# First five ticks of a two-stage mixture-of-experts kernel written out one by one, its opening loads issued two at a time

## The reference

```python
x = x + _L0_xattn_ref(_layernorm(x), itok, ctx, ctx, ctx)   # stage 1
x = x + _L0_ffn_ref(_layernorm(x), router_w, wg, wu, wd)    # stage 2
```

## Time and profile before

| what | value |
|---|---|
| median of three runs | 255.06 us |
| the profiled execution's own time | 255.76 us |
| its span, first to last instruction | 253.8 us |
| TensorE, busy share of the span | 92% |
| VectorE, ScalarE, GpSimd, busy share | 86%, 83%, 65% |

### The profile page before, as it was taken

How to read it: one execution, slowest core, us unless ns; L and a number is a source line. 1 busy time by engine, 2 the same in 40 slices (tenths; PEclk the granted TensorE clock), 3 DMA queues, 4 the chain that set the end, 5 groups by cost and what they waited for, 6 DMA issues and landing times.

```text
span 253.8 us, 5722 instructions
## 1 busy us (share of the span) xinstructions
PE 234.7 (92%) x1409; PEld 172.4 (68%) x1419; DVE 218.2 (86%) x675; ACT 210.5 (83%) x324; POOL 164.2 (65%) x325
## 2 busy tenths in 40 slices
PE   2398999999999999999999999999999999999990
PEld 2255778888888888888888888886455555555530
DVE  5879989899889988799888988879999999999871
ACT  2767899799888988898888888787899999999960
POOL 4362665868778777588777664347538786757653
PEclk9999999999999999999999999999999999999996
DMA  5999944935754499784566534541388962211110
GB/s 203 425 359 362 424 180 151 362 131 226 243 210 146 134 354 406 283 324 157 201 249 227 147 127 169 207 146 69 98 237 250 310 251 85 83 41 68 70 37 0
DMA packets 13726, 51.71 MB, mean 204 GB/s; under 512 B 2750, under 2 KB 2750, under 8 KB 10112
## 3 DMA queue, kind: packets, MB, share of 16 engines
q1 hardware_dynamic: 8816, 37.91, 42.4%
q0 software_dynamic: 4880, 13.44, 14.4%
HBM read 40.49 MB, written 13.48 MB: 213 GB/s over the span
## 4 chain that ended last, share of the span: by engine, by line
PE 73%; DVE 10%; DMA 9%; issue 4%; ACT 1%; POOL 1%; SPq 0%; DVEq 0%; ACTq 0%
PE bank L1555 33%; PE bank L1677 19%; PE bank L1539 9%; PE bank L1647 5%; DMA staged<-weight_chunks 4%; PE bank L1669 4%; DMA ternary<-weight_chunks 3%; PE bank L1784 2%; DMA staged<-x_rows 1%; DVE ternary L957 1%; DVE ctx_lo L1000 1%; PE bank L1574 1%; POOL out_rows L643 1%; DVE ternary L1019 1%; DMA token_ids<-token_ids_in 1%
## 5 line engine op out<-in xcount | busy, mean ns | idle before, releaser
L1677 PE MATMUL bank<-ternary,qT 128*128 x179 | 43.6, 380 | 0.5
L694 ACT ACTIVATE ternary<-staged 128x2048 bf16<-128x2048 f32 x20 | 38.0, 1899 | 2.5 <-DMA staged<-weight_chunks 2.5
L700 ACT ACTIVATE ternary<-staged,w_scale 128x1536 int16<-128x1536 f32 x20 | 31.4, 1576 | 2.3 <-DVE w_scale L1014 0.6
L1677 PEld LDWEIGHTS bank<-ternary,qT 128*128 128x128 bf16 x184 | 17.7, 97 | 20.2 <-issue 5.4
L562 POOL DMA_INDIRECT x_rows<-row,store_at x19 | 25.5, 1340 | 6.8 <-POOL store_at L554 5.0
L643 POOL DMA_INDIRECT out_rows<-late_rows,late_token x18 | 19.0, 1057 | 9.4 <-DVE late_rows L1350 8.0
L473 POOL DMA_INDIRECT x<-x_rows,gather x16 | 18.5, 1155 | 10.2 <-DVE gather L969 6.3
L1677 PE MATMUL bank<-ternary,rT 128*128 x87 | 22.6, 380 | 0.4 <-ACT rT L812 0.2
L747 ACT ACTIVATE p<-bank,rstd 128x512 f32<-128x512 f32 x19 | 13.0, 684 | 11.6 <-PE bank L1555 11.5
L1555 PE MATMUL bank<-ctx_hi,pT_hi 128*128 x76 | 22.3, 415 | 0.1
L1555 PE MATMUL bank<-ctx_hi,hT_hi 128*128 x76 | 22.3, 414 | 0.0
(11 more groups left out here) (237 smaller groups left out, 658.6 us busy)
## 6 DMA issues: line engine op xcount, KB each, us to landing
staged<-weight_chunks SPq DMA_DIRECT2D x20, 1024.0 KB, 5.5
late_rows<-x_rows SPq DMA_DIRECT2D x18, 260.0 KB, 3.7
ternary<-ctx_chunks SPq DMA_DIRECT2D x4, 1024.0 KB, 8.3
ternary<-weight_chunks SPq DMA_DIRECT2D x4, 1024.0 KB, 9.8
x_rows<-filler SPq DMA_DIRECT2D x1, 2080.0 KB, 12.9
staged<-x_rows SPq DMA_DIRECT2D x5, 260.0 KB, 2.7
x_rows<-row,store_at POOLq DMA_INDIRECT x19, 6.0
out_rows<-late_rows,late_token POOLq DMA_INDIRECT x18
```

Of the source, the lines that this page charges most:

```text
L694: nc.scalar.activation(ternary[:, m * K * D:(m + 1) * K * D], staged_of(i), ACT.Abs, accum_out=abs_sum[:, 2 * i:2 * i + 1]).then_inc(abs_r ...
L700: nc.scalar.activation(ternary[:, m * K * D + DVE_COLS:(m + 1) * K * D].bitcast(I16), staged_of(i)[:, DVE_COLS:], ACT.Copy, scale=w_scale[ ...
L1677: last = pe.matmul(ps[:, :], left[:, k * P:(k + 1) * P], ternary[:, bass.ds(e * (3 * K * D) + (kind * K + k) * D, D)], start=(k == 0), sto ...
```

## The change

The loops of TensorE, VectorE and ScalarE now start at t = 5 (`OPENING`). What they did for t = 2 to 4, and blocks 0 and 1, stands written out in a new order. On TensorE other work is put between the parts of a product, by a table `ahead` from part number to a function. Blocks 0 to 3 (`b < E1`, E1 = 4) now wait for `hT_lo` only at the third part; block 4 and later still wait at the start. `second_product(0)` waits for the low half of pT only at its third part. SP waits until context 2 has landed before it issues matrix 3, and until matrix 2 has landed before context 3. One warm-up matmul of 12 is dropped. GpSimd's list is unchanged. No arithmetic is added or removed.

```diff
-WARM_UP = (9, 3)
+WARM_UP = (8, 3)
+OPENING = 5
...
             load_context(2)
             load_weights(2)
+            sp.wait_ge(ctx_in_sem[2], 16)
             load_weights(3)
+            sp.wait_ge(staged_early_in[0], 16)
             load_context(3)
...
# ScalarE
-            sum_abs(1)
             evict_hT(0)
             scale_part(0)
+            sum_abs(1)
+            evict_hT(1)
+            silu(0)
+            sum_abs(2)
+            evict_pT(0)
             scale_part(1)
...
-            for t in range(2, TICKS):
+            for t in range(OPENING, TICKS):
...
# VectorE, from block 2's statistics on
+            moments_of(2)
+            aggregate(2)
+            normalise(2)
+            gate(0)
+            hT_rest(1)
+            mean_of(1)
+            scale_of(1)
+            low_half(2, 0)
...
+            cut(4)
+            residual(2)
+            negative_mean(2)
+            scale_part(5)
+            hT_rest(4)
+            largest(1)
+            top_logits(1)
...
# TensorE
-                    if n == 1 and b == 1:
+                    if n == 1 and b is not None and 1 <= b < E1:
                         pe.wait_ge(ctx_lo_ready, e + 1)
-                    if n == 2 and b in (0, 1):
+                    if n in ahead:
+                        ahead[n]()
+                    if n == 2 and b is not None and b < E1:
                         pe.wait_ge(hT_lo_ready, b + 1)
...
-                if b < 2:
+                if b < E1:
                     pe.wait_ge(hT_hi_ready, b + 1)
...
                 else:
                     pe.wait_ge(hT_lo_ready, b + 1)
...
+            def in_second2():
+                rank(0)
+                sum_mean(5)
+                transpose_h(4)
+            second_product(2, {2: in_second2})
+            transpose_p(3)
+
+            def in_first4():
+                logits(1)
+            first_product(4, {2: in_first4})
+            load_expert(5)
+            count_in(0)
+            transpose_x1(2)
+            transpose_h(5)
+            rank(1)
+            sum_mean(6)
+            second_product(3)
+            logits(2)
+            count_in(1)
+            for t in range(OPENING, B1):
```

More of the change, by code:

```diff
@@ L1360, in _ @@
             normalise(0)
-            variance(0)
             low_half(0, 1)
[L1363 to L1366, removed]
+            scale_of(0)
             moments_of(1)
@@ L1369, in _ @@
             normalise(1)
+            hT_rest(0)
+            variance(0)
             variance(1)
-            scale_part(0)
-            gate(0)
-            hT_rest(1)
+            low_half(1, 0)
             low_half(1, 1)
-            scale_part(1)
-            pT_rest(0)
             moments_of(2)
@@ L1379, in _ @@
             normalise(2)
+            gate(0)
[3 more added lines that the diff above has]
+            low_half(2, 0)
             variance(2)
-            low_half(2, 0)
-            gate(1)
+            scale_part(0)
+            pT_rest(0)
+            low_half(2, 1)
             mean_of(2)
             scale_of(2)
-            hT_rest(2)
-            low_half(2, 1)
-            scale_part(2)
+            gate(1)
             moments_of(3)
             aggregate(3)
+            residual(0)
+            negative_mean(0)
+            hT_rest(2)
+            normalise(3)
             variance(3)
+            scale_part(1)
+            moments_of(4)
+            mean_of(3)
+            scale_of(3)
+            aggregate(4)
+            pT_rest(1)
+            gate(2)
+            low_half(3, 0)
+            low_half(3, 1)
+            mean_of(4)
+            scale_part(2)
+            scale_of(4)
+            residual(1)
+            negative_mean(1)
+            hT_rest(3)
+            scale_part(3)
+            scale_part(4)
+            top_logits(0)
+            choice(0)
+            one_hot(0)
+            pT_rest(2)
+            normalise(4)
+            largest(0)
+            moments_of(5)
+            variance(4)
+            mean_of(5)
+            gate(3)
+            scale_of(5)
+            row_index(0)
+            aggregate(5)
+            variance(5)
+            cut(4)
+            residual(2)
+            negative_mean(2)
+            scale_part(5)
+            hT_rest(4)
+            largest(1)
+            top_logits(1)
+            choice(1)
+            one_hot(1)
+            normalise(5)
+            pT_rest(3)
+            largest(2)
+            gate(4)
+            mean_of(6)
+            scale_of(6)
+            scale_part(6)
+            row_index(1)
+            hT_rest(5)
+            moments_of(6)
+            aggregate(6)
+            variance(6)
+            cut(5)
             early, factors = early_slots(), mean_products()
-            for t in range(2, TICKS):
+            for t in range(OPENING, TICKS):
                 interlude = early if t == EARLY_AFTER + 4 else iter(())
@@ L1583, in transpose_h, with first_product @@
                 transpose1(hT_ps, h).then_inc(hT_ready, 1)
[L1585 removed]
+            def first_product(b, ahead={}):
                 if not 0 <= b < B1:
                     return
[L1588 removed]
+                if b < E1:
                     pe.wait_ge(hT_hi_ready, b + 1)
[L1591 removed]
+                    pe.wait_ge(*((ctx_hi_ready, b + 1) if b < 2 else (pool_hi_ready, b - 1)))
                     pe.wait_ge(centred, 1)
```

104 lines of the change are left out of this document (63 added, 41 removed).

## The result

The changed kernel takes 260.87 us (median of four runs, 259.94 to 261.83) against 255.34 us before (four runs, 254.93 to 255.88): a ratio of 1.0215, 95% interval 1.0165 to 1.0265. It is slower, by some 2%. 255.5 us was forecast, with 256.7 as the upper end.

What follows compares the result with a forecast made beforehand. TensorE was taken as the bound, VectorE as a nearly full second; the start of tick 5 fixes the time. +0.3 and +0.15 give +0.45 us: 255.76 to 256.2 profiled, 255.5 us as median, range 254.3 to 256.7.

Steps and rivals of the forecast that it cites:

- VectorE from 21.7 to `pT_rest(2)`: VectorE's operations from block 2's statistics on: 17.1 us, plus 1.1 and 0.8 of waits, giving 40.7 us.
- two h 0.80: Within VectorE's stretch from 21.7 us: two normalises (h) counted at 0.80 us together, a step of 0.40 from block 0's row.
- the clock: Slower rival, chance 0.05: TensorE idle at block 4 or after warm-up loses its high clock, 2.5 us more, 258 us.
- The gap of 0.78 us cost nothing: Evidence against a clock fall: TensorE's 0.78 us gap for p of block 0 in the kernel before cost nothing.
- VectorE reaches block 2 at 21.7: VectorE's walk up to block 2: the statistics of block 2 are reached at 21.7 us.
- the first rival: Slower: block 2's x lands as late as before, at 22.8, costing 1.1 us, 256.6; chance 0.22 with late matrix 2.
- x of block 2 in time: Gather 2 lands between 17.6 and 22.8 us, wanted at 21.7; taken as in time, nearer to gather 0's 4.5 us.
- The gap at block 4, 2.05 us: TensorE idle 2.05 us at block 4's first product, waiting for `hT_lo`, which VectorE has behind block 2's residual; start at 47.45.
- From block 4 to tick 5, 8.41 us: TensorE from block 4's first product to tick 5's transposition of p: 7.60 plus 0.81 for one more set of logits.
- TensorE's wait for `pT_rest(1)`, 0.5 us: TensorE, ahead of the old order before block 4, stands 0.5 us for VectorE's `pT_rest(1)`.
- The store: Slower rival, chance 0.08: first store leaves at about 51 us, block 3's residual waits for it; 1.3 us more, 256.8.
- +0.45 us: Net delay of tick 5: +0.3 us (55.9 against 55.60) plus 0.15 for the walk coming early.

Runs made afterwards that it cites:

- experiment 2: Changed kernel with the normalise of block 2 alone written as a tensor_tensor with the mean broadcast, in place of a tensor_scalar: ratio 1.0147.
- experiments 1 and 4: The run of experiment 1, and the changed kernel without SP's two new waits (259.89 us, ratio 1.0137); the kernel before with those waits alone had ratio 1.0007.
- experiment 7: Kernel of ratio 0.9972 with one edit taken back: cast behind normalise 256.79 us, or block 4 piece by piece 257.66 us (its profiled execution 261.73).
- the cast edit: GpSimd's cast of context 2 made to wait for VectorE's normalise of block 2; alone on the changed kernel ratio 1.0228, also used in later runs.
- experiment 3: Changed kernel with eight warm-up matmuls into an unused bank ahead of the first transposition of p: 258.98 us, ratio 1.0144.
- experiment 1: Changed kernel with GpSimd's cast of context 2 made to wait for VectorE's normalise of block 2: ratio 1.0228, four runs from 259.31 to 480.93 us.
- the second kernel of experiment 6: Changed kernel with delayed cast, block 4 piece by piece, first store earlier, block 4's statistics later, and three more moves on VectorE and ScalarE: ratio 0.9993.

## Why the prediction was wrong

**The step that failed** is "VectorE from 21.7 to `pT_rest(2)`", in the term "two h 0.80". I took the step of a normalise from block 0's row, where GpSimd was doing nothing, and walked GpSimd's list only for its own delays. The h of block 2 took 2.83 us instead of 0.49. GpSimd's cast is let go by the second low half of context 1. Before, a scaling, a low half of p, statistics and an aggregate stood between that and the normalise (24.52 to 26.45), and the cast was nearly over; in the new order only statistics and an aggregate do (21.93 to 22.87). The cast was let go at 22.02 (19.67 + 2.35, the end of that low half) and began at 23.51, because gather 3 and a root stood ahead of it on GpSimd. The prediction saw that delay, put it at 2.2 us where its own starts (16.3 and 19.4) give 3.1 and the traces 3.45 (gather 3 at 18.06 and 21.51), and asked only when the gather's data is wanted, not what the delay puts the cast beside. The trace of the kernel before had the sign of it: a normalise of 0.59 us at a cast's end, the rows under experiment 2. It is only 0.1 us, but the one row where the two engines met.

**The rival with too small a chance** is the clock: 5% and 258 us. Its mechanism is what happened, behind a gap that I hadn't foreseen, and in part of the runs behind the one that I had. "The gap of 0.78 us cost nothing" was true and no ground for 5%, as the stretch that was read had no gap of two microseconds. Its price, 2.5 us, lies between those measured: some 1.8 us in the changed kernel, 1.6 in experiments 1 and 4 (10.18 and 10.20 us from block 4 to tick 5, for 8.62), 3.2 in experiment 7. The Trainium skill (TensorE: Matmul & The Clock Gate, Part 1) said that idleness brings the half rate back; the rows of the changed kernel now show it.

Term by term, for the rest:

- *VectorE reaches block 2 at 21.7*: 21.93, without a wait for a load. Right. In six of the experiments' traces VectorE did wait for x of block 2 there, 0.20 to 0.49 us, so the first rival was near.
- *x of block 2 in time*: gather 2, issued at 13.10, landed after 7.7 us, at 20.8. The first rival did not happen, though not because a gather behind two loads is as fast as gather 0 (4.5 us). Matrix 2 was taken up at 22.52 without a wait.
- *The gap at block 4, 2.05 us*: 2.04 us, at the row named, released by `hT_lo`.
- *VectorE's wait for the largest logits, 2.4 us*: 2.48 us.
- *From block 4 to tick 5, 8.41 us*: 59.90 - 51.28 = 8.62.
- *TensorE's wait for `pT_rest(1)`, 0.5 us*: none in the changed kernel, whose TensorE came late; 0.40 to 2.18 us in five of the six traces with the cast edit.
- *The store*: issued at 54.69, not 51, but landed after 3.5 us; no residual waited.
- *+0.45 us*: no run has the new order without any of these costs, so it stays unproven. It fits two accounts. In the changed kernel 0.45 forecast + 2.34 held + 1.8 clock = 4.6, of which 4.30 arrived. In experiment 3, where the clock stayed, tick 5 began at 58.37, 2.77 us late, for 0.45 + 1.87 held (2.36 - 0.49) + 0.39 of waiting for x of block 2 = 2.71.

The sum also hid something that the experiments brought out: even with the cast out of the way, the new order stays at a ratio of 1.005 to 1.007 as long as either block 4 waits for the whole of `hT_lo` or its statistics stand ahead of `pT_rest(1)`. What the order wins ahead of block 3 is given back there, the first part as the forecast said; with the fall of the clock behind block 4's gap, that is why undoing the one unforeseen cost alone (experiment 1) left the time nearly where it was.

## What to carry to other kernels

When a change reorders one engine's list, lay the lists of VectorE and GpSimd side by side over the new order: a duration read from a row holds only beside the same neighbour. When one such meeting is undone, look for the next of its kind (here the cast of context 3). Price an idle stretch of TensorE with its fall of the clock, one or more of them, even where the rows before have no such gap. And when one cost is undone and the time doesn't move, look in the trace for how far the gain got (here to 49.07 us) before the theory is dropped.

## What the runs showed of the hardware

- A 128x512 normalise of VectorE from SBUF to SBUF took 2.83, 2.74, 2.55, 2.36 and 2.25 us beside a cast of GpSimd that began behind it, 0.59 to 1.72 us where it began 0.3 us or more before the end of a running cast, and 0.49 beside a gather's issue and a root of one column. In all of these that met a cast it ended 0.27 to 0.29 us after the cast. The form with two inputs in SBUF took 3.11 us.
- A scaling that began 0.15 us ahead of a cast took its usual 0.48 us, and the cast 2.09 us in place of 1.89 to 1.91; one that began beside a running cast took 1.07 us (the second kernel of experiment 6).
- Whether the clock falls behind an idle stretch of TensorE of 1.6 to 2.2 us is not settled by its length. Nine of the profiled executions have twelve such stretches between 12 and 62 us. It fell behind six (1.72, 1.77, 2.03, 2.03, 2.04 and 2.11 us) and not behind the other six (1.63, 2.04, 2.04, 2.04, 2.10 and 2.18 us). A fall cost 1.6 to 1.8 us, once 3.2.
- The same gather of 128 rows (block 4) landed after 4.0 to 6.7 us where SP asked for the next matrix 3.2 to 3.5 us behind it, and after 7.6 to 8.6 us where it asked 1.6 us or less behind it.
